# Two directions' decay matrices summed before one product, and a new order of a Mamba layer's last stages

## What is computed

```python
dt = softplus(dt + dt_bias)                     # step size per token and head, both directions
xBC = silu(conv(xBC)); x, B, C = split(xBC)     # heads: 8, head size 64, state 128
def ssd(x, A, B, C, chunk):                     # called with x * dt and A * dt, chunk = 128
    A_cs   = cumsum(A)                          # within a chunk
    Lmat   = segsum_exp(A)                      # exp of the sum of A from j+1 to i, 0 for i < j
    Y_diag = einsum('bcln,bcsn,bhcls,bcshp->bclhp', C, B, Lmat, x)
    states = einsum('bcln,bhcl,bclhp->bchpn', B, exp(A_cs[-1] - A_cs), x)   # then run over chunks
    Y_off  = einsum('bcln,bchpn,bhcl->bclhp', C, states, exp(A_cs))
    return Y_diag + Y_off
y  = shifted(ssd forward + x * D) + shifted back(ssd backward + x * D) + x * (x @ fc_D.T + D)
yg = y * silu(z)
out = (yg * rsqrt(mean(yg ** 2) + eps) * norm_w) @ out_proj.T
```

## Time and profile before

| what | value |
|---|---|
| median of 3 runs | 1984.8 us (1983.58 to 1989.7) |
| the profiled execution | 1983.85 us, span 1982.2 us |
| busy over the span | PE 1776.8 (90%), DVE 1379.6 (70%), ACT 1185.7 (60%), POOL 429.3 (22%) |
| Mamba's sequences | `near` starts first at 119.9, last at 610.6 |
| L1041, products of `L` with `xdt` | 124.7 us in 1024 records (each product has two) |
| L1365, `L` times `masked` on DVE | 101.8 us, 64 of 1609 ns on the mean |
| L1166, exponentials on ACT | 153.1 us, 512 of 387 ns on the mean |

### The profile page before, as it was taken

How to read it: one execution, slowest core, us unless ns; L and a number is a source line. 1 busy time by engine, 2 the same in 40 slices (tenths; PEclk the granted TensorE clock), 3 DMA queues, 4 the chain that set the end, 5 groups by cost and what they waited for, 6 DMA issues and landing times. The chain is left out here.

```text
span 1982.2 us, 33791 instructions
## 1 busy us (share of the span) xinstructions
PE 1776.8 (90%) x10009; PEld 1227.8 (62%) x10090; DVE 1379.6 (70%) x3026; ACT 1185.7 (60%) x2870; POOL 429.3 (22%) x406
## 2 busy tenths in 40 slices
PE   5689999999999799999578879999989898989897
PEld 2456766676676689999433455656556464656555
DVE  3867887877788222222256978888879797888885
ACT  5256666566556222122154448887888888888886
POOL 2032442353244304321120120110202010020101
PEclk9789999999999999999789979999999999999999
DMA  5511222222121496554284752242425232343311
GB/s 177 191 54 64 95 95 73 80 101 74 63 95 64 174 318 204 196 180 148 83 283 134 213 164 75 78 83 76 107 76 107 70 90 62 84 98 85 88 27 33
DMA packets 149694, 226.12 MB, mean 114 GB/s; under 512 B 17613, under 2 KB 118095, under 8 KB 149424
## 3 DMA queue, kind: packets, MB, share of 16 engines
q1 hardware_dynamic: 132928, 189.39, 31.1%
q0 software_dynamic: 16624, 35.01, 7.3%
HBM read 174.26 MB, written 50.99 MB: 114 GB/s over the span
## 5 line engine op out<-in xcount | busy, mean ns | idle before, releaser
L2390 DVE TENSOR_SCALAR att_scores<-att_psS 128x512 f32<-128x512 f32 x512 | 349.1, 682 | 95.8 <-PE att_psS L2220 57.4
L2339 ACT ACTIVATE att_prob<-att_scores,att_shift 128x512 f32<-128x512 f32 x512 | 383.6, 749 | 24.4 <-DVE att_shift L2406 24.3
L2348 ACT COPY att_pT<-att_psT 128x512 f32<-128x512 f32 x512 | 306.3, 599 | 134.3 <-PE att_psT L2228 133.5
L2398 DVE CUSTOM_DVE_ANT_0 att_scores<-att_scores,first_decay 128x512 f32<-128x512 f32 x512 | 347.9, 680 | 0.0
L2228 PEld LDWEIGHTS att_psT<-ident,att_prob 128*128 128x128 f32 x2048 | 244.3, 141 | 158.8 <-issue 98.2
L2228 PE MATMUL att_psT<-ident,att_prob 128*128 128x128 f32 x2048 | 314.4, 277 | 19.4 <-ACT att_pT L2348 16.0
L2220 PE MATMUL att_psS<-first_ks,first_qs 128*128 128x512 bf16 x431 | 165.0, 384 | 15.5 <-DVE att_scores L2390 13.2
L2242 PE MATMUL att_psO<-att_pT,att_v 128*32 128x512 f32 x1024 | 139.2, 618 | 42.3 <-ACT att_pT L2348 37.9
L1614 ACT ACTIVATE ffn_hT<-ffn_psH,ffn_b 128x128 f32<-128x128 f32 x156 | 44.6, 368 | 194.2 <-PE ffn_psH L1570 194.1
L1166 ACT ACTIVATE mamba_L<-mamba_am,mamba_minus 128x128 f32<-128x128 f32 x512 | 153.1, 387 | 0.1
L1570 PE MATMUL ffn_psH<-ffn_xT,ffn_w 128*128 128x128 f32 x1248 | 146.1, 275 | 6.0 <-DMA ffn_w<-in_w 5.4
(11 more groups left out here) (314 smaller groups left out, 2850.5 us busy)
## 6 DMA issues: line engine op xcount, KB each, us to landing
ffn_w<-in_w SPq DMA_DIRECT2D x47, 1024.0 KB, 5.8
mamba_am<-a_rows SPq DMA_DIRECT2D x64, 512.0 KB, 3.8
first_qs<-q_parts SPq DMA_DIRECT2D x256, 64.0 KB, 3.0
first_ks<-k_parts SPq DMA_DIRECT2D x256, 64.0 KB, 3.1
xn<-xn_all SPq DMA_DIRECT2D x16, 512.0 KB, 6.0
att_w<-in_inter POOLq DMA_DIRECT2D x7, 1024.0 KB, 5.5
att_w<-in_outer POOLq DMA_DIRECT2D x7, 1024.0 KB, 6.8
q_parts<-proj_parts SPq DMA_DIRECT2D x8, 768.0 KB, 4.1
```

The lines of the kernel that those rows point to most:

```text
L2339: nc.scalar.activation(prob[:, n % NP], scores[:, n % NCL], ACT.Exp, bias=shift[:, h % 2, t:t + 1], accum_out=total[:, octet % 2, t, j, i: ...
L2348: nc.scalar.copy(pT[:, h % HEADS_T, :, t * P:(t + 1) * P], bank_of("turn", n)[:].rearrange("p (k q) -> p k q", k=CPB)).then_inc(pT_ready, 1)
L2390: vec.tensor_scalar(scores[:, n % NCL], psS[n % NS][:], -CLAMP, CLAMP, ALU.max, ALU.min).then_inc(clipped, 1)
L2398: vec.tensor_tensor_reduce(scores[:, n % NCL], scores[:, n % NCL], decay[:, FAR - t * P:FAR - t * P + SEQ], 1.0, -2.0 * CLAMP, ALU.mult, A ...
```

## The change

Four things change in the Mamba stage, and one in the stage ahead.

1. The step size dt goes into the exponent (as its logarithm, `lw`, added to `minus` in the stage ahead, with one more logarithm on ACT and one more maximum on DVE). So `xdt` and its eight POOL products per sequence go away, and so does the copy `dtb`.
2. DVE adds the two directions' finished `L` into one (a new 128x1024 addition per tile), and PE multiplies the sum by `xl`: 8 products per tile in place of 16. `L` has six buffers, not four.
3. ACT makes all eight units' exponentials one after the other, ahead of `squares(0)`.
4. DVE's and PE's orders are new: on DVE tiles 0 and 1's decays stand ahead of `grow(2)`; the reading of `psY` (`take_tile`) is apart from `finish`; on PE `neighbours`, `diagonal` and `off` are apart. The product with the gate z goes from DVE to POOL (`gate`).

Core of the diff:

```diff
@@ stage ahead, DVE
+                v.tensor_scalar(w[:], steps.dt[:], LEAST_NORMAL, None, ALU.max).then_inc(floored, 1)
...
-                v.tensor_copy(steps.minus..., psM...).then_inc(minus_ready, 1)
+                dve.wait_ge(logged, 2)
+                v.tensor_tensor(steps.minus..., psM..., lw..., ALU.add).then_inc(minus_ready, 1)
@@ Mamba, PE
+                    def diagonal(t):
+                        pe.wait_ge(L_ready, i * CPB + t + 1)
+                        for h in range(NH):
+                            mm = nc.tensor.matmul(psY[t % 2][:, h * HD:(h + 1) * HD], L[:, 2 * t % NL, h], xl[:, t, h * HD:(h + 1) * HD],
+                                                  start=False, stop=(h == NH - 1), skip_group_check=True)
+                        mm.then_inc(diag_used, 1)
+                    def off(t):
+                        pe.wait_ge(state_ready, (i + 1) * 6)
+                        for d in range(2):
+                            if (d == 0 and t > 0) or (d == 1 and t < CPB - 1):
+                                done = max(2 * t - 2 + d, 0) if t else 0
+                                pe.wait_ge(off_scaled, i * 6 + done)
+                                lo = t * P + (0 if d == 0 else 2)
+                                nc.tensor.matmul(psO[d][:], xc[:, 5 + 2 * d, lo:lo + P], state[:, d, t],
+                                                 start=True, stop=True).then_inc(off_ready, 1)
@@ Mamba, PE's order behind grow(2)
+                    neighbours(0)
                     diagonal(0)
+                    products(2)
+                    neighbours(1)
+                    diagonal(1)
+                    off(0)
+                    off(1)
+                    products(3)
+                    neighbours(2)
+                    diagonal(2)
+                    off(2)
+                    turn_tile(0)
+                    neighbours(3)
+                    output(0)
+                    diagonal(3)
+                    off(3)
+                    turn_tile(1)
+                    output(1)
                     turn_tile(CPB - 2)
@@ Mamba, ACT
-                    for u in range(NL):
+                    for u in range(U):
                         decays(i, u)
-                    decays(i, 4)
                     squares(i, 0)
-                    decays(i, 5)
                     turned_tile(i, 0)
@@ Mamba, POOL
+                    def gate(t):
+                        pool.wait_ge(summed, i * CPB + t + 1)
+                        nc.gpsimd.tensor_tensor(y[:, t % 2], y[:, t % 2], zs[:, t], ALU.mult).then_inc(gated, 1)
+                    skip_rows(0)
+                    skip_rows(1)
+                    gate(0)
+                    skip_rows(2)
+                    rms(0)
+                    gate(1)
+                    skip_rows(3)
+                    rms(1)
+                    gate(2)
+                    rms(2)
+                    gate(3)
+                    rms(3)
@@ Mamba, DVE
+                    def decays(t):
...
+                        for d in range(2):
+                            u = 2 * t + d
+                            dve.wait_ge(decayed, i * U + u + 1)
+                            v.scalar_tensor_tensor(out=L[:, u % NL], in0=L[:, u % NL], scalar=LARGE,
+                                                   in1=masked[:, t % 2, d].unsqueeze(1).to_broadcast([P, NH, P]),
+                                                   op0=ALU.min, op1=ALU.mult).then_inc(L_masked, 1)
+                        dve.wait_ge(L_masked, i * U + 2 * t + 2)
+                        v.tensor_tensor(L[:, 2 * t % NL], L[:, 2 * t % NL], L[:, (2 * t + 1) % NL], ALU.add).then_inc(L_ready, 1)
@@ Mamba, DVE's order
                     decays(0)
-                    decays(1)
                     (fd)
+                    decays(1)
                     grow(2)
+                    take_tile(0)
+                    decays(2)
                     count = 0
+                    for t in range(CPB):
+                        count = off(2 * t, count)
+                        count = off(2 * t + 1, count)
+                        if t:
+                            take_tile(t)
+                        finish(t)
+                        if t == 1:
                             decays(3)
+                        elif t >= 2:
+                            outputs(t - 2)
```

119 lines of the change are left out of this document (36 added, 83 removed).

## The result

The changed kernel takes **2000.79 us** (median of 5 runs, 1995.03 to 2004.98) against 1985.18 us for the kernel before (5 runs, 1983.58 to 1989.7): ratio 1.0076, 95% interval 1.0053 to 1.01. It is 15.6 us slower. The forecast was 1994 us, 1977 to 2006, with 0.62 on slower. The profiled execution took 2004.98 us (span 2003.3, granted clock 0.942 on the mean), 4.2 us above the median of its runs; before it was 1983.85, with 0.963.

The account below looks back on a forecast made before the run. It took the chain through DVE's sums to the next convolution on PE as the bound. 7 × (1.05 + 0.5) − 1.8 + 0.4 = +9.4 on 1983.85 gives 1993.3, as a median 1994 us; range 1977 to 2006.

Parts of the forecast that it names:

- a tail that has moved behind the last sum: PE's work from tile 3's sum to the next convolution: products, state product, transposes, tile 1's `output`; sum at 369.8, convolution 376.0.
- the walk: Step-by-step timeline of one Mamba sequence, 342.08 to 374.96, new orders with old durations; chance 0.55, own range 1988 to 2001.
- the forecast signs: Expected in the changed profile: `near` period 71 to 71.8, addition 1.22, `L` times `masked` near 1.8 or 1.22, more clock falls.
- no change: Rival: milder POOL meetings or a clock that hardly falls; +0.4 per sequence, 1985 to 1990, chance 0.15.
- faster: Rival: POOL's gates and skips do not disturb DVE; convolution 0.4 to 1.1 earlier, 1976 to 1981, chance 0.13.
- PE is the bound: Rival: PE, 97% busy, limits the sequence and its 7 us are gained; 1936, chance 0.05.
- Rival (1): PE's clock stays low from the waits at 344 and 350; +3 to +3.5 per sequence, 2006 to 2010, chance 0.12.
- old falls: Clock falls in the last two whole sequences of the kernel before, 1.8 us in all, dropped from the sum.
- the term +1.05 per sequence: Next convolution on PE starts at 376.0 against 374.96, from the longer chain of DVE and PE.
- a meeting: Two DVE `L` products beside two POOL products cost DVE 1.35; two per sequence, taken as 1.4 (tile 1) and 1.5 (tile 3).
- The wait at the third state product: PE stands from about 356.6 until 360.1 for DVE's first `off` to empty its PSUM bank, 3.5 us.
- +0.8 in two of three, +0.5 on the mean: Clock falls around 360 delay the third state product, DVE's second `off` and PE's chain; us per sequence.

Follow-up runs that it names:

- experiment 6: Changed kernel with POOL's `skip_rows` cut to the first of eight heads, the other heads' skip term left out: 1980.04 us, ratio 0.9976.
- experiment 8: Changed kernel plus the edits of 1 and 5, with `skip_rows` moved from POOL to ACT as eight scaled copies per tile: 1973.9 us, ratio 0.9932.
- the edits of 1 and 5: On the changed kernel: PE's tile 1 transposes ahead of tile 3's products (1991.72 us); added to that, DVE's `outputs(0)` ahead of `take_tile(2)` (1988.21 us).
- experiment 7: Kernel before with only dt put into the exponent, no `xdt`; old orders, 16 products per tile and gate on DVE kept: 1969.77 us, ratio 0.992.
- experiment 9: Changed kernel without the sum of the two directions, PE making 16 products of `L` per tile: 1979.8 us, ratio 0.9975.
- experiment 3: Changed kernel with 33 unread idle products per sequence added on PE where it waits for DVE: 1994.2 us, ratio 1.0049.
- experiment 4: Changed kernel with the gate product back on DVE instead of POOL: 2005.62 us, ratio 1.0101.
- experiment 2: Changed kernel with DVE's first `off` and tile 0's `finish` ahead of tile 2's decays: 2023.5 us, ratio 1.0196.

## Why the prediction was right, and where its sizes were off

**Direction and mechanism held.** "7 us less of PE's work ends as waits plus a tail that has moved behind the last sum": the waits stand where the walk had them, though two of them are shorter, and in the undisturbed sequence DVE has no wait from tile 0's `masked` to tile 3's sum. Of the forecast signs, the period (71 to 71.8) is right for four of seven; the addition is 1224 ns against 1.22; `L` times `masked` falls into 1.9 and 1.2. The rivals "no change", "faster" and "PE is the bound" fell; experiment 6, and experiment 8 with the edits of 1 and 5 in it, show that the condition of "faster" was the right one: with POOL's skips out of DVE's way the kernel is below before. Rival (1)'s 2006 to 2010 leaves out the 1.8 us of old falls that the sum drops; with them it is 2004 to 2008.

**What the change is made of.** By undisturbed periods: dt in the exponent takes 69.84 to 67.6 (experiment 7), the new orders with the gate on POOL take it to 69.9 (experiment 9), the sum of two directions to 71.4 (the changed kernel), and the lower clock adds 0.9 on the mean. So, taken in this order, the sum costs 2.4 a sequence with its clock and the new orders cost 2.3.

**The chain was right to 0.5 us.** Less 7.2, the profile has tile 1's sum done at 351.9 (walk 351.9), the first `off` done at 360.0 (360.05), tile 3's sum at 370.1 (369.8), PE's wait for it 0.96 (1), the convolution at 376.5 (376.0). So **the term +1.05 per sequence was mis-sized, it measured +1.5**. Ahead of the sum it is +0.3: tile 3's `masked` starts at 364.3 (walk 364.15), as the sum of the two `yo` took 0.88 beside POOL, and tile 3's two `L` took 3.95, a meeting of 1.6 over 2.36 where I took 1.5; in it stands POOL's gate, which took 1.27 where I had 1.04. Behind it, the tail to the convolution took 6.4 where the walk has 6.2, with `output(1)` waiting 0.77 for ACT's copy.

The three meetings shown are 1.35, 1.45 (tile 1) and 1.59 (tile 3). By the rule of the Trainium skill, "SBUF — State Buffer", section "SBUF: two separate sides", worked out as in the prediction from the same rows (what is left of POOL's first product when DVE's first `L` starts, plus 1.04 for the second), they would cost, as estimates, 1.66, 0.74 + 1.04 = 1.78 and 0.88 + 1.04 = 1.92. Each measured one is 0.3 below: the rule follows the growth from one meeting to the next, and so worked out is 0.3 too high.

**The wait at the third state product was 1.6, not 3.5.** The end of it is where I put it, the start is not: by my walk PE had nothing to do from 356.6. The profile shows the two state products ahead of it at the lower clock even in the undisturbed sequence: they begin at 361.96 − 7.2 = 354.8, as in the walk, and take 3.68 us, where one took a pitch of 0.9 and the last 1.08 in the earlier trace rows. So the work itself filled that time. In the same way PE's wait before tile 1's products was 0.83 and not 2: the neighbours ahead of them had taken 1.9. The lower clock cost nothing there, but it is the same fact that made the next term wrong.

**The clock is the other term that was mis-sized.** I took "+0.8 in two of three, +0.5 on the mean". Measured are three of seven periods longer by 1.7 to 2.9, 0.9 on the mean, and experiment 3, with the clock held up in six of seven periods, has those six undisturbed. I had reasoned that at the lower clock the work fills gaps; it does, up to tile 2, but in the two 73.1 us sequences DVE waits 0.57 for PE (224.9) and PE reaches tile 3's sum 1.4 us after it is ready. That is rival (1), true in two sequences of seven. The third, 74.3 us, is neither my term nor that rival: its fall lies behind the last sum, in the tail, where my walk had every piece of work at the full clock and nothing beside it that could hide a slower one.

**What was luck.** With 1.5 and 0.9 the sum of the prediction would have been 7 × 2.4 − 1.8 + 0.4 = 15.4, so 1999 on the profiled execution and 2000 as a median, close to the measured 2000.79. But the 0.9 comes from one execution, the longest of five, and the share of the clock changes from one to the next: the two executions at 0.946 took 1995, the one at 0.939 took 2004.86. The walk's own range ended at 2001, 0.2 above the measured median, and the forecast change of 9 us was too small by 6.

**What I did not ask.** I summed the change as one. Experiment 7 shows that it has a part that gains 16 us (dt in the exponent: no `xdt` products, and no `L` disturbed any more); a walk for that part alone was not done ahead of the result. The one made later, ahead of experiment 7, had the direction and 0.8 to 1.5 a sequence, where 2.2 was measured. The "faster" rival was tied to POOL's `gate` and `skip_rows` not disturbing DVE; that `xdt` had been disturbing it all along stood in the earlier trace rows.

**Open.** How the 2.3 us per sequence between experiments 7 and 9 divide between the new order and the gate (experiment 4 says that the gate alone, in the joined kernel, is a gain of up to 0.9); what in experiment 7 the vanished meetings bring and what the vanished products and copy do; and what makes a period of the changed kernel one of 71.4 or one of 73 to 74, as the instructions are the same.

## What to carry to other kernels

An engine that is busy for 97% of a period is not the bound if its work can't start earlier: walk the chain from the last unchanged event to the next, with the durations of the trace, and do it for each part of the change apart, since a gain and a loss can hide in one. Before a step is moved earlier on DVE, list what it releases on POOL and what DVE does at that time: experiment 2 lost 23 us by that. Work taken from an engine that then waits in short pieces can cost twice, once in the waits and once in its clock; compare the same instruction's duration on either side before you count the saving.
